# Seven stage boundaries of a twelve-layer decoder kernel joined: a stage's last norm, output and projection run inside the next stage

## The chip, the cores and the metric

The kernel runs on one core of a Trainium2 chip. The metric is device time in microseconds (us) of one execution, smaller is better. One execution was recorded by the hardware profiler. Its rows carry the time in us from the start of the recorded span.

## The reference, cut to what matters

Twelve sublayers follow each other on x, 32 sequences (batch) of 128 tokens with 128 channels, float32. Each is "x = layernorm(x + f(x))".

```python
x = _layernorm(x + _L0_ffn_ref(x, ...))      # stage 2, slots
x = _layernorm(x + _L1_attn_ref(x, ...))     # stage 3, linear attention over the batch axis
x = _layernorm(x + _L1_xattn_ref(x, ctx_768, ...))  # stage 4, 8 heads of 64
x = _layernorm(x + _L1_ffn_ref(x, ...))      # stages 5 and 5.5: rope attention, then 8 gated experts
x = _layernorm(x + _L2_attn_ref(x, ...))     # stage 6, relu attention
x = _layernorm(x + _L2_xattn_ref(x, ctx_768, ...))  # stage 7, 16 heads of 8, with an MLP
x = _layernorm(x + _L2_ffn_ref(x, ...))      # stage 8, 8 linear experts, top 2
x = _layernorm(x + _L3_attn_ref(x, ...))     # stage 9, rope attention, 16 heads of 64
x = _layernorm(x + _L3_xattn_ref(x, ctx_768, ...))  # stage 10, 16 heads of 8
x = _layernorm(x + _L3_ffn_ref(x, ...))      # stage 11, 8 gelu experts
```

Stages 0 (attention) and 1 (cross attention with a convolution) come ahead of these and are not touched. Except for stage 3, which mixes over the batch axis, and for gates that stage 11 takes from means over a sequence, a stage treats each sequence by itself: its first pair of sequences needs nothing of the last pair of the stage before.

## The kernel before, in words

All of x stays on the chip in the tile `X`, 128 partitions by 32 sequences by 128. The engines work through a stage in units: a pair of sequences (index p, 16 pairs) in `attention8`, `attention64_rope`, `attention64_cross` and `experts_gated`, four sequences (index u or v, 8 units) in `slots`, `attention_linear`, `attention_relu`, `experts_linear` and `experts_gelu`. One function writes one stage: stage 2 is `slots`, 3 `attention_linear`, 4 `attention64_cross`, 5, 7 and 10 `attention8`, 5.5 `experts_gated`, 6 `attention_relu`, 8 `experts_linear`, 9 `attention64_rope`, 11 `experts_gelu`. (In the profile tile names have lost their number: L_ffn is any of L0_ffn to L3_ffn, so the time tells the stage.)

The order of work is written out by hand. Each stage opens a block (`nc.Block()`), and in it one Python function for each engine issues that engine's instructions in program order, with waits on semaphores where another engine's result is needed. An engine runs strictly through its own list. Inside a stage the loops are software pipelined: while TensorE (PE) does unit u, the output of unit u-1 goes through residual, statistics, root and normalisation. The typical end of a unit is: PE projects the output, VectorE (DVE) adds the residual (`residual`) and takes mean and variance (`statistics`), GpSimd (POOL) takes the reciprocal root (`root`, `normed`), and either POOL writes X, or DVE makes the shift (`shifted`) and ScalarE (ACT) writes X (`block_out`). The event `x_out` counts the written units.

At the end of a block all engines meet. Then `Signals.new_stage` (L52) clears the semaphores and has a second meeting (`all_engine_barrier`, L56), the stage's memory is given back, and the next stage begins with nothing in flight. Its head is: PE transposes the first unit of X (`turn`), ACT moves the transposed unit from PSUM (`evict_x`), PE projects it, and so on. Stages 3 and 4 are already joined: they lie in one block with semaphores and memory of both, stage 3's tail (`TurnedTail`) is issued inside stage 4.

Weights lie in two buffers that alternate by stage. The queue of SyncE (SP) loads the next stage's weights during a stage (`load_weights`, L379): at the stage's start in most, but in stages 2, 3 and 6 only when the stage's last output projection is done:

```python
            def _(sp):
                sp.wait_ge(y_ps, UNITS)
                k.load_weights(sp, k.next_stage(stage))
```

so that the weights of stage 3 and of stage 7 are fetched at the very end of stages 2 and 6.

## Time and profile before

| | us |
|---|---|
| median of 3 runs | 3188.23 |
| lowest and highest | 3179.7, 3191.69 |
| profiled execution, its own time | 3196.24 |
| its recorded span | 3194.4 |
| PE busy (31745 matmuls) | 2708.6, 85% of the span |
| DVE busy | 1930.6, 60% |
| ACT busy | 1378.5, 43% |
| POOL busy | 1366.7, 43% |
| TensorE clock granted, mean of the span | 0.897 of full speed |

How to read it: busy time is summed over the engine's instructions; the granted clock has two levels, 0.5 (1.2 GHz) and 1.0 (2.4 GHz), and a mean lies between. The profiled execution lasted 8 us longer than the median run. "SPq" is the queue from which transfers are started, and in a row of the timeline the last bracket says how long the engine had been idle and what ended that.

### The profile page before, as it was taken

What the parts mean: (1) busy time and instruction counts of PE and PEld (TensorE: products, weight loads), DVE (VectorE), ACT (ScalarE), POOL (GpSimd) and SP (SyncE); (2) the same over time, 40 slices, a digit from 0 to 9 for tenths busy, and PEclk for the clock granted to TensorE, in tenths of its full rate; (3) what the DMA queues carried; (4) which work ended last, traced back from release to release, by engine and by line L of the source; (5) the groups of instructions that cost most, each with busy time, mean ns of one, the idle gap of its engine ahead of it and who ended that gap; (6) DMA issues with size and microseconds to landing.
All of it is one profiled execution on the core that took longest, in us unless ns stands there. A gap on an engine that the chain in (4) does not pass through costs nothing. (4 is left out here: it accounts for less than half of the span.)

```text
span 3194.4 us, 78319 instructions
## 1 busy us (share of the span) xinstructions
PE 2708.6 (85%) x31745; PEld 1921.9 (60%) x31745; DVE 1930.6 (60%) x5041; ACT 1378.5 (43%) x3100; POOL 1366.7 (43%) x1474
## 2 busy tenths in 40 slices
PE   7884666676689997998999976998889999979986
PEld 4552343354446775665999965666367777755665
DVE  6887999255764444665544444664856666635665
ACT  4453565263445653444322223553134444435554
POOL 4773665173301213453233333453833434335556
PEclk8996776687779998999899986997989999989998
DMA  3000000400000001000000000001000000000000
GB/s 105 2 2 1 1 1 1 117 1 1 7 19 17 2 2 41 2 3 9 1 1 1 1 1 17 2 2 44 1 6 2 2 3 2 2 9 2 2 3 25
DMA packets 25797, 37.16 MB, mean 12 GB/s; under 512 B 760, under 2 KB 22656, under 8 KB 24576
## 3 DMA queue, kind: packets, MB, share of 16 engines
q1 hardware_dynamic: 25440, 32.16, 3.3%
q8 instruction: 254, 4.16, 0.6%
q14 instruction: 103, 0.84, 0.1%
HBM read 29.93 MB, written 2.23 MB: 10 GB/s over the span
## 5 line engine op out<-in xcount | busy, mean ns | idle before, releaser
L1460 POOL TENSOR_TENSOR L_attn__qk<-L_attn__turned 128x512 f32<-128x512 f32 x128 | 161.7, 1274 | 303.1 <-DVE L_attn__turned L1571 303.1
L1024 DVE TENSOR_REDUCE L_xattn__nm<-psum 128x8 bf16<-128x1024 f32 x128 | 156.4, 1224 | 148.8 <-PE psum L1225 142.4
L4510 PE MATMUL psum<-L_ffn__e_hT,weights 128*128 128x256 f32 x1024 | 244.7, 382 | 0.0
L1571 DVE TENSOR_TENSOR L_attn__turned<-psum,weights 128x1024 f32<-128x1024 f32 x128 | 153.3, 1218 | 95.1 <-PE psum L1678 92.1
L4510 PEld LDWEIGHTS psum<-L_ffn__e_hT,weights 128*128 128x128 f32 x1024 | 186.7, 192 | 20.5
L4364 DVE TENSOR_TENSOR L_ffn__e_a<-L_ffn__e_sg,psum 128x512 f32<-128x512 f32 x128 | 88.0, 687 | 176.5 <-ACT L_ffn__e_sg L4356 176.4
L4356 ACT ACTIVATE L_ffn__e_sg<-psum 128x512 f32<-128x512 f32 x128 | 76.4, 597 | 258.7 <-PE psum L4510 258.7
L959 ACT ACTIVATE L_xattn__pT<-psum 128x1024 f32<-128x1024 f32 x128 | 124.0, 1021 | 59.3 <-PE psum L1253 59.3
L4523 PEld LDWEIGHTS psum<-weights,L_ffn__e_a 128*128 128x128 f32 x1024 | 134.3, 191 | 7.3 <-DVE L_ffn__e_a L4364 0.7
L1678 PE MATMUL psum<-L_attn__xT,weights 128*128 128x256 f32 x512 | 136.8, 401 | 2.0 <-DVE L_attn__turned L1571 1.3
L4523 PE MATMUL psum<-weights,L_ffn__e_a 128*128 128x128 f32 x1024 | 135.1, 275 | 0.5 <-DVE L_ffn__e_a L4364 0.5
L1506 ACT ACTIVATE L_attn__qk<-L_attn__qk 128x512 bf16<-128x512 f32 x128 | 77.3, 630 | 87.7 <-POOL L_attn__qk L1460 87.7
L4283 POOL TENSOR_TENSOR L_ffn__e_half<-L_ffn__e_prod 128x512 f32<-128x512 f32 x32 | 40.7, 1270 | 171.6 <-DVE L_ffn__e_prod L4373 171.6
L1024 DVE TENSOR_REDUCE L_ffn__nm<-psum 128x8 bf16<-128x1024 f32 x64 | 78.2, 1224 | 55.5 <-PE psum L1225 55.5
L954 ACT ACTIVATE L_attn__pT<-L_attn__pT,L_attn__sc 128x1024 f32<-128x1024 f32 x64 | 73.0, 1149 | 76.4 <-DVE L_attn__pT L1036 76.4
L1678 PEld LDWEIGHTS psum<-L_attn__xT,weights 128*128 128x128 f32 x512 | 90.9, 193 | 24.4 <-issue 9.9
L3040 DVE MATCH_REPLACE8 L_xattn__front_left<-L_xattn__front_top,L_xattn__front_left 128x128 f32<-128x128 f32 x384 | 100.8, 275 | 0.0
L1024 DVE TENSOR_REDUCE L_attn__nm<-psum 128x8 bf16<-128x1024 f32 x64 | 77.9, 1220 | 29.1 <-PE psum L1225 29.1
L1580 DVE TENSOR_REDUCE L_attn__nm<-psum 128x8 bf16<-128x1024 f32 x64 | 75.4, 1219 | 26.5 <-PE psum L1709 25.8
L3182 PE MATMUL psum<-L_xattn__front_diag,L_xattn__front_ex 128*128 128x128 f32 x256 | 55.6, 388 | 40.0 <-POOL L_xattn__front_ex L2869 38.7
L1529 ACT ACTIVATE L_attn__pT<-psum 128x1024 f32<-128x1024 f32 x64 | 62.0, 1021 | 62.1 <-PE psum L1738 62.1
L1900 POOL TENSOR_TENSOR L_xattn__rstd<-L_xattn__mv,eps 128x2 f32<-128x2 f32 x16 | 3.1, 194 | 198.4 <-DVE L_xattn__mv L2029 198.4
(682 smaller groups left out, 7562.1 us busy)
## 6 DMA issues: line engine op xcount, KB each, us to landing
L_xattn__conv_toeplitz<-s4d_kernel SPq DMA_DIRECT2D x5, 1024.0 KB, 12.1
weights<-pack SPq DMA_DIRECT2D x1, 3328.0 KB, 11.0
weights<-pack SPq DMA_DIRECT2D x1, 3140.0 KB, 10.1
weights<-s4d_kernel SPq DMA_DIRECT2D x3, 1024.0 KB, 9.2
L_attn__bias_tables<-pack SPq DMA_DIRECT2D x1, 2048.0 KB, 10.1
out_dram<-X SPq DMA_DIRECT2D x8, 256.0 KB, 2.3
weights<-pack SPq DMA_DIRECT2D x1, 1603.5 KB, 14.1
ctxT<-ctxT_in SPq DMA_DIRECT2D x1, 1536.0 KB, 11.0
```

What stands on the lines that cost most here:

```text
L959: nc.scalar.activation(unit, scores[u], ACT.Exp, scale=scale).then_inc(p_sb, 1)
L1024: nc.vector.tensor_reduce(nm[:, n % 2, :].rearrange("p (g c) -> p g c", g=4)[:, 2 * u:2 * u + 2, 0:4], scores[u].rearrange("p g (i q) -> p ...
L1460: nc.gpsimd.tensor_tensor(qk[:, p % 2, u], turned[:, g % 2, :, 0:2 * P], turned[:, g % 2, :, 2 * P:4 * P], ALU.add).then_inc(qk_sb, 1)
L1506: nc.scalar.activation(qk16[:, p % 2, u], qk[:, p % 2, u], ACT.Copy).then_inc(qk16_sb, 1)
L1571: nc.vector.tensor_tensor(turned[:, g % 2], proj[u % 2].unsqueeze(1).to_broadcast([P, 2, 4 * P]), k.w(name + "rope").rearrange("p (t q) -> ...
L1580: nc.vector.tensor_reduce(nm[:, n % 2, :].rearrange("p (g c) -> p g c", g=4)[:, 2 * u:2 * u + 2, 0:4], scores[u].rearrange("p g (j q) -> p ...
L1678: last = nc.tensor.matmul(proj[place % 2][:, 2 * P * t:2 * P * t + 2 * P], w[:, P * c:P * c + P], xT[:, p % 2, :], start=True, stop=True)
L3040: last = nc.vector.match_replace(left[:, u % 2, j, h, :], top[:, u % 2, j, h, 8 * r:8 * r + 8], source(u, r, j, h), 2 * NEG)
L4356: nc.scalar.activation(sg[:, g % 2, :], gate[g % 2], ACT.Silu).then_inc(sg_sb, 1)
L4364: nc.vector.tensor_tensor(a[:, g % 2].rearrange("p c s q -> p (c s q)"), sg[:, g % 2, :], up[g % 2], ALU.mult).then_inc(a_sb, 1)
L4510: last = nc.tensor.matmul(bank[g % 2][:, 256 * c:256 * c + 256], k.w(name + w)[:, o:o + P], hT, start=True, stop=True)
L4523: last = nc.tensor.matmul(Y[s][e // 4][:, P * (e % 4):P * (e % 4) + P], a[:, g % 2, c, s, :], k.w(name + "Wd")[:, P * (2 * e + c):P * (2 * ...
```

## The change

Three blocks now hold the stages: 2, 3 and 4; 5, 5.5, 6 and 7; 8, 9, 10 and 11. That joins seven boundaries: 2 to 3, 5 to 5.5, 5.5 to 6, 6 to 7, 8 to 9, 9 to 10 and 10 to 11. Those from 1 to 2, 4 to 5 and 7 to 8 keep their meetings. A joined stage returns an object `Ending` with its last piece of work for each engine as functions (`late_pe`, `late_dve`, `last_dve`, `late_act`, `late_pool`), and the next stage calls them at chosen places in its own lists. `Ending` also says on what the next stage must wait: `x_out` for a unit of X (`wait_x`), `banks_read` before it writes PSUM banks that the old stage still uses, `weights_read` before SP loads over the old weights. All waits on a unit of X are new in these stages. Memory of successive stages is taken from alternate ends (`other_end`), so that both stages' tiles can be alive; some tiles are declared in another order for that. In `experts_linear` two PSUM banks are chosen otherwise, with one more wait.

```diff
+    def other_end(self):
+        self.end = "right" if self.end == "left" else "left"
+        return self.end
...
-            return ctx.enter_context(nc.sbuf_tensor(f"{name}_{what}", shape, dt))
+            return ctx.enter_context(nc.sbuf_tensor(f"{name}_{what}", shape, dt, side=side))
...
+class Ending:
+    def __init__(self, x_out, pairs_each, weights_read, banks_read=None):
+        self.x_out, self.pairs_each, self.weights_read, self.banks_read = x_out, pairs_each, weights_read, banks_read
+
+    def wait_x(self, eng, pair):
+        eng.wait_ge(self.x_out, pair // self.pairs_each + 1)
...
@@ attention8 (stages 5, 7, 10) @@
                 nc.gpsimd.memset(nm[:], 0.0)
                 nc.gpsimd.memset(vz[:], 0.0).then_inc(zeroed, 1)
+                if before:
+                    before.late_pool(pool)
                 pool.wait_ge(k.loaded[stage], 16)
...
                 evict_v(0)
+                if before:
+                    before.late_act(act)
                 evict_x(1)
...
                     nc.vector.tensor_copy(bvw[:], k.w(name + "bv").to_broadcast([P, P])).then_inc(bv_sb, 1)
+                    if before:
+                        before.late_dve(dve)
                     dve.wait_ge(bv_ps, 1)
...
                 project_v(0)
-                if opening:
+                if before:
+                    before.late_pe(pe)
+                    pe.wait_ge(*before.banks_read)
+                if opening or before:
                     value_bias()
                 turn(1)
...
+                def late_pe(pe):
+                    if mlp:
+                        hide(LAST, LAST + 1)
+                    project_out(LAST, LAST + 1)
...
@@ attention64_rope (stage 9) @@
                 nc.gpsimd.memset(nm[:], 0.0).then_inc(zeroed, 1)
                 for u in range(UNITS):
+                    if u == 4:
+                        before.late_pool(pool)
                     add_turned(0, u)
...
                 for u in range(UNITS):
                     cast(0, u)
+                before.late_act(act)
+                act.wait_ge(before.x_out, NB // 4)
                 for i in range(4):
                     evict_v(0, i)
...
@@ attention_linear (stage 3) @@
                 for u in BY_ACT:
+                    if u == 5:
+                        before.late_act(act)
...
                 for u in BY_DVE:
+                    if u == 2:
+                        before.last_dve(dve)
...
@@ attention_relu (stage 6) @@
                 biased(0)
+                before.late_dve(dve)
...
@@ experts_gated (stage 5.5) @@
                 for u in range(UNITS):
                     rms_root(u)
+                    if u == 1:
+                        before.late_pool(pool)
...
+                before.late_dve(dve)
                 for u in range(UNITS):
                     rms_normed(u)
+                    if u == 0:
+                        before.last_dve(dve)
...
                 pe.wait_ge(k.loaded[stage], 16)
+                before.late_pe(pe)
                 turn(0)
...
@@ experts_gelu (stage 11) @@
-                for u in range(UNITS):
+                turn(0)
+                before.late_pe(pe)
+                for u in range(1, UNITS):
                     turn(u)
...
@@ the stages @@
         with k.one_block():
-            tail = attention_linear(k, 3, "L1_attn_")
+            ending = slots(k, 2, "L0_ffn_")
+            tail = attention_linear(k, 3, "L1_attn_", ending)
             attention64_cross(k, 4, "L1_xattn_", tail)
+        with ExitStack() as mid, k.one_block():
+            M = mid.enter_context(nc.sbuf_tensor("L1_ffn_mid", [P, NB, DM], F32))
+            ending = attention8(k, 5, "L1_ffn_", grouped=M, followed=True)
+            ending = experts_gated(k, 5.5, "L1_ffn_", M, ending)
+            ending = attention_relu(k, 6, "L2_attn_", ending)
+            attention8(k, 7, "L2_xattn_", cross=True, mlp=True, before=ending)
+        with k.one_block():
+            ending = experts_linear(k, 8, "L2_ffn_")
+            ending = attention64_rope(k, 9, "L3_attn_", ending)
+            ending = attention8(k, 10, "L3_xattn_", cross=True, before=ending, followed=True)
+            experts_gelu(k, 11, "L3_ffn_", ending)
```

On POOL at the boundary from stage 9 to stage 10, the list before (the first five rows write the last pair of X, `nm` and `vz` are tiles of stage 10, `k16m` is the first operand that its scores need):

```order
L1466 TENSOR_TENSOR L_attn__rstd<-L_attn__mv,eps 128x2
L1468 TENSOR_TENSOR L_attn__rstd<-L_attn__rstd,neg_half 128x2
L1472 TENSOR_SCALAR X<-L_attn__res,L_attn__mv,L_attn__rstd 128x128 x2
L1446 UNCONDITIONAL_BRANCH
L55 ISA
L776 UNCONDITIONAL_BRANCH
L848 MEMSET L_xattn__nm 128x256
L849 MEMSET L_xattn__vz 128x2560
L783 TENSOR_TENSOR L_xattn__k16m<-L_xattn__kT,const 128x1024
```

and now:

```order
L773 UNCONDITIONAL_BRANCH
L847 MEMSET L_xattn__nm 128x256
L848 MEMSET L_xattn__vz 128x2560
L1505 TENSOR_TENSOR L_attn__rstd<-L_attn__mv,eps 128x2
L1507 TENSOR_TENSOR L_attn__rstd<-L_attn__rstd,neg_half 128x2
L1511 TENSOR_SCALAR X<-L_attn__res,L_attn__mv,L_attn__rstd 128x128 x2
L780 TENSOR_TENSOR L_xattn__k16m<-L_xattn__kT,const 128x1024
```

The zeroing has moved ahead of the old stage's last norm, and `k16m` still stands behind that norm.

On PE at the same boundary, before (`rd` is the old stage's last reciprocal, spread out; `oT` its last output):

```order
L1768 MATMUL psum<-L_attn__rd,weights 128x128 x8
L1775 MATMUL psum<-weights,L_attn__oT 128x128 x8
L1446 UNCONDITIONAL_BRANCH
L1149 UNCONDITIONAL_BRANCH
L1313 MATMUL psum<-weights,L_xattn__bvw 128x128
L1160 MATMUL psum<-const,X 128x128 x2
L1172 MATMUL psum<-ctxT,weights 128x256
L1173 MATMUL psum<-L_xattn__xT,weights 128x256
L1199 MATMUL psum<-weights,ctxT 128x128 x2
L1160 MATMUL psum<-const,X 128x128 x2
```

and now:

```order
L1828 MATMUL psum<-L_attn__rd,weights 128x128 x8
L1171 UNCONDITIONAL_BRANCH
L1184 MATMUL psum<-const,X 128x128 x2
L1196 MATMUL psum<-ctxT,weights 128x256
L1197 MATMUL psum<-L_xattn__xT,weights 128x256
L1223 MATMUL psum<-weights,ctxT 128x128 x2
L1835 MATMUL psum<-weights,L_attn__oT 128x128 x8
L1337 MATMUL psum<-weights,L_xattn__bvw 128x128
L1184 MATMUL psum<-const,X 128x128 x2
```

The old stage's last projection (reading `oT`) has moved behind the new stage's first transposes and projections.

On ACT at the boundary from stage 8 to stage 9, before:

```order
L4629 ACTIVATE L_ffn__wT<-psum 32x128
L4634 ACTIVATE X<-L_ffn__r,L_ffn__shift,L_ffn__rstd 128x128 x12
L4578 UNCONDITIONAL_BRANCH
L1493 UNCONDITIONAL_BRANCH
L1500 ACTIVATE L_attn__xT<-psum 128x256
L1506 ACTIVATE L_attn__qk<-L_attn__qk 128x512 x8
L1512 ACTIVATE L_attn__v<-psum 128x512 x4
```

and now:

```order
L4789 ACTIVATE L_ffn__wT<-psum 32x128
L4794 ACTIVATE X<-L_ffn__r,L_ffn__shift,L_ffn__rstd 128x128 x4
L1538 UNCONDITIONAL_BRANCH
L1545 ACTIVATE L_attn__xT<-psum 128x256
L1551 ACTIVATE L_attn__qk<-L_attn__qk 128x512 x8
L4794 ACTIVATE X<-L_ffn__r,L_ffn__shift,L_ffn__rstd 128x128 x8
L1557 ACTIVATE L_attn__v<-psum 128x512 x4
```

Eight writes of X, two units of stage 8, now stand between the casts of `qk` and the moves of `v` out of PSUM.

## Rows read from the trace of the kernel before

**Rows 1.** Windows, seven boundaries: stretch, us; busy PE, PEld, DVE, ACT, POOL; PEclk, DMA, GB/s

```profile
849.10:855.30 6.20, 0.00 (x0) 0.02 (x1) 2.00 (x10) 2.95 (x8) 1.24 (x3) 0.50 0.28 77
1502.50:1512.30 9.80, 0.69 (x5) 0.56 (x5) 3.78 (x8) 3.72 (x24) 3.54 (x6) 0.72 0.19 54
1871.30:1882.60 11.30, 0.00 (x0) 0.00 (x0) 4.25 (x12) 0.00 (x0) 7.33 (x10) 0.68 0.00 0
1965.00:1971.40 6.40, 0.00 (x0) 0.00 (x0) 2.35 (x11) 2.66 (x7) 1.70 (x4) 0.50 0.30 82
2309.10:2321.30 12.20, 0.01 (x1) 0.04 (x1) 4.84 (x14) 3.29 (x8) 6.34 (x9) 0.63 0.00 1
2854.00:2864.90 10.90, 3.79 (x17) 3.49 (x17) 2.41 (x6) 1.09 (x2) 2.99 (x6) 0.55 0.00 0
3068.30:3076.40 8.10, 0.69 (x5) 0.55 (x5) 3.31 (x7) 0.00 (x0) 2.80 (x5) 0.82 0.00 0
```

**Rows 2.** Window, the boundary from stage 3 to 4, joined already

```profile
967.40:977.40 10.00, 7.69 (x39) 5.28 (x38) 5.14 (x17) 6.23 (x14) 3.87 (x6) 1.00 0.12 51
```

**Rows 3.** Timeline, stage 2 to 3: start us, us, engine line op out<-in xcount [idle before <-releaser]

```profile
849.12 0.34 SPq L383 DMA_DIRECT2D weights<-pack  x1
...
852.59 1.65 ACT L3748 ACTIVATE X<-L_ffn__r,L_ffn__shift,L_ffn__rstd 128x128 f32<-128x128 f32 x4 [2.19 <-DVE L_ffn__shift L3912]
...
857.35 4.65 ACT L2530 ACTIVATE L_attn__HT<-psum,weights 128x128 f32<-128x128 f32 x16 [3.12 <-PE psum L2671]
```

**Rows 4.** DMA issues, weights of stage 7 and of stage 3: KB, us to landing

```profile
weights<-pack SPq DMA_DIRECT2D x1, 514.5 KB, 3.5
...
weights<-pack SPq DMA_DIRECT2D x1, 469.0 KB, 3.7
```

**Rows 5.** Timeline, stage 5 to 5.5, DVE

```profile
1502.57 1.76 DVE L1043 RECIPROCAL L_ffn__rd<-psum 128x256 f32<-128x256 f32 x1 [3.23 <-PE psum L1275]
...
1511.01 2.42 DVE L4409 SCALAR_TENSOR_TENSOR L_ffn__e_xn<-L_ffn_mid,L_ffn__e_ms,weights 128x128 f32<-128x128 f32 x8 [4.94 <-POOL L_ffn__e_ms L4314]
```

**Rows 6.** Timeline, stage 5.5 to 6: DVE's last residual, and PE's first state product

```profile
1877.28 0.29 DVE L4383 TENSOR_TENSOR L_ffn__e_total<-L_ffn__e_moe,L_ffn_mid 128x128 f32<-128x128 f32 x1 [1.22 <-POOL L_ffn__e_moe L4291]
...
1890.79 1.16 PE L2383 MATMUL psum<-L_attn__kv,L_attn__kr 128*128 128x128 f32 x8 [1.18 <-POOL L_attn__kr L2228]
```

**Rows 7.** Timeline, stage 6 to 7: SP's two loads of weights, PE's first transposes

```profile
1964.99 6.25 SPq L383 DMA_DIRECT2D weights<-pack  x2
...
1972.30 0.67 PE L1160 MATMUL psum<-const,X 128*128 128x128 f32 x2
```

**Rows 8.** Timeline, stage 8 to 9: POOL's last sum, its last first-pair add, ACT's moves of v

```profile
2313.68 0.73 POOL L4594 TENSOR_TENSOR L_ffn__quarter<-L_ffn__half 128x256 f32<-128x256 f32 x1
...
2335.57 1.26 POOL L1460 TENSOR_TENSOR L_attn__qk<-L_attn__turned 128x512 f32<-128x512 f32 x1 [0.18 <-DVE L_attn__turned L1571]
...
2337.40 1.06 ACT L1512 ACTIVATE L_attn__v<-psum 128x512 f32<-128x512 f32 x2
```

**Rows 9.** Timeline, stage 9 to 10: last projection, last write of X, first k16m

```profile
2856.09 3.78 PE L1775 MATMUL psum<-weights,L_attn__oT 128*128 128x128 f32 x16 [2.09 <-DVE L_attn__oT L1596]
...
2861.93 1.57 POOL L1472 TENSOR_SCALAR X<-L_attn__res,L_attn__mv,L_attn__rstd 128x128 f32<-128x128 f32 x2
...
2869.46 1.89 POOL L783 TENSOR_TENSOR L_xattn__k16m<-L_xattn__kT,const 128x1024 bf16<-128x1024 f32 x1 [2.51 <-ACT L_xattn__kT L910]
```

**Rows 10.** Timeline, stage 10 to 11: last write of X, and the step behind the last transpose

```profile
3073.79 1.57 POOL L813 TENSOR_SCALAR X<-L_xattn__res,L_xattn__mv,L_xattn__rstd 128x128 f32<-128x128 f32 x2
...
3084.22 0.18 DVE L4920 TENSOR_SCALAR L_ffn__pooled<-L_ffn__total 128x32 f32<-128x32 f32 x1
```

**Rows 11.** Windows: router of stage 5.5, transposes of stage 11

```profile
1522.00:1536.00 14.00, 14.00 (x60) 13.28 (x61) 7.15 (x65) 4.94 (x14) 1.99 (x3) 0.50 0.00 1
...
3076.40:3080.30 3.90, 3.90 (x18) 3.29 (x19) 1.72 (x3) 1.91 (x4) 0.00 (x0) 0.50 0.00 0
3080.30:3082.80 2.50, 2.37 (x16) 1.49 (x14) 2.29 (x5) 2.27 (x4) 0.00 (x0) 1.00 0.00 0
```

314 lines of the change are left out of this document (192 added, 122 removed).

## The prediction

> **What bounds the kernel now.** I read the page's busy times first: PE works 85% of the span and no other engine more than 60%, so over most of the time an interruption of PE is lost time. I then laid the timeline over each place where one stage ends and the next begins, and asked the view by windows how much PE does there. [rows 1] gives the seven stretches that the change touches, from the end of PE's main work in the old stage to PE's start in the new one. They last 6.2, 9.8, 11.3, 6.4, 12.2, 10.9 and 8.1 us, 64.9 us together, and PE works 5.2 us of them. The reader should see that the other engines work only about a third of each stretch too: what fills it is a chain, in which each engine waits for the one before it. These 60 idle us are 1.9% of the time, and they bound what bridging can give. The boundary from stage 3 to stage 4, joined already, looks otherwise: in the 10 us around it PE works 7.69 us, at full clock [rows 2].
>
> **The change, boundary by boundary.** It removes no arithmetic. It removes two meetings at each boundary, and puts the old stage's last chain beside the new stage's first unit. The time from the last write of X to the new stage's start is what the meetings cost: 852.59 + 1.65 = 854.24 to 855.3 [rows 1, 3], so 1.0 us, and about the same at each, 7 us in all. The rest depends on which wait ends last in the new head. I follow each head to the first step that the following work hangs on, with its old durations, and compare.
>
> *2 to 3.* PE can begin its transposes at 849.1 instead of 855.3. But stage 3's weights are asked for only at 849.12 [rows 3] and take 3.7 us [rows 4], so ACT and DVE, which wait for them before they take anything from PSUM, start at 852.8. ACT has 4 units of 4 moves, 4.65 us [rows 3], and now the last write of X, 1.65 us, between its second and third. It ends at 852.8 + 4.65 + 1.65 = 859.1 instead of 862.0. **2.9 us.** Before, this load was hidden by the chain and the meetings; now it is what comes last.
>
> *5 to 5.5.* The reciprocal ends at 1504.33 [rows 5], the product after it takes some 0.4 us, and then DVE does the new stage's first unit, 4 of the 8 operations in 2.42 us, 1.2 us [rows 5]. PE transposes from 1506.0 or 1506.1 instead of 1512.3 [rows 1]. The second DVE unit has the residual ahead of it (0.4 us), and POOL's third root has the old stage's last clip (about 1 us) ahead. From 6.2 us I take those off in part: **5.5 us.**
>
> *5.5 to 6.* PE is free at 1871.3 and nothing in stage 6's first unit needs the last pair. Before, PE began at 1882.6 [rows 1] and reached the product that needs POOL's result at 1890.79 [rows 6], 8.2 us later. Now that is 1879.5. A second limit is POOL, which is busy with the old stage's expert sums until the time at which DVE takes them, 1877.28 [rows 6], and then needs some 1.5 us for the new stage's positive part: 1878.8, not later. DVE's old residual waits for the same sums, but stands behind the bias of unit 0. **11.3 us**, the whole stretch.
>
> *6 to 7.* Stage 7's weights are asked for at 1964.99 [rows 7] and take 3.5 us [rows 4]. PE waits for them even ahead of its first transposes, which stood at 1972.3 (some 0.2 us earlier by their weight load) and now stand at 1968.5. The old last residual on DVE also waits for these weights now, since it stands behind DVE's wait, but by my estimate root and write are done by 1977, about where the shifted head next needs ACT. **3.6 us.**
>
> *8 to 9.* PE has nothing late and starts at 2309.1. POOL is the brake: its expert sums end at 2314.41 [rows 8], and only then come the first pair's eight adds, 1.26 us each [rows 8], which feed ACT's casts. In the old head they ran to 2336.83, about 10.9 us from the first start (their turned operands come from DVE at the same pace). DVE's late residual and statistics fall between its fourth and fifth, which I price at 2.5 us, half of what DVE does in the stretch [rows 1]. So the adds end at 2314.8 + 10.9 + 2.5 = 2328.2, 8.6 us earlier. Then ACT has two units of X to write, 2 x 1.65 us by [rows 3], before it moves v, on which PE waits. Before, they had been written ahead of the stage. 8.6 - 3.3 = **5.3 us.**
>
> *9 to 10.* This is the place where most is given back. PE starts the new head at 2854.0. In the old head the step `k16m` on POOL came at 2869.46 [rows 9], 4.6 us after PE's start at 2864.9 [rows 1]; so the operands would be there at 2858.7. But PE now does the old projection here, 3.78 us, to 2862.5, and from the end of that projection to the end of POOL's write of X it took 2859.87 to 2863.50, 3.6 us [rows 9]. POOL has that norm ahead of `k16m`, which therefore starts at 2866.1 instead of 2869.46. **3.4 us** out of 10.9.
>
> *10 to 11.* Stage 11 needs all of X, transposed, before its gates. The last pair is still written at 3075.36 [rows 10], but now all other transposes are done by then. Last transposes 1 us, ACT's move 0.6, DVE's sum 0.7 and small gaps: the pooled mean at 3077.9 instead of 3084.22 [rows 10]. **6.3 us.** The rest of stage 11 is shifted as it is.
>
> Sum: 2.9 + 5.5 + 11.3 + 3.6 + 5.3 + 3.4 + 6.3 = **38.3 us**. The added waits (on X, banks and weights) mostly find their event past, and queue nothing but what is counted above. SP's wait on `weights_read` in stages 5.5, 7, 9 and 10 moves loads by a few us that are needed one stage later, 80 us and more away; I cost it at nothing. So do I cost the other memory ends, the tiles' order and the other banks of stage 8: no address appears in a row, and the arithmetic is the same. Against the profiled execution the sum gives 3196.24 - 38.3 = 3157.9 us. That execution stands 8.0 us over the median, so the forecast is 3188.23 - 38.3 = **3150 us**.
>
> **The clock, the cost that the sum leaves out.** The mean granted clock in the seven stretches is 0.50 to 0.82 [rows 1], and it is where 0.5 is 1.2 GHz. In the router of stage 5.5 PE is busy for all of 14 us at 0.5 [rows 11], so the idle stretch ahead is not all that holds it down. At the joined boundary it is 1.0 [rows 2]. If the bridging keeps the clock up, a head's PE time halves at best: 14 us become 7 there. From both sides: nothing gained (the old durations hold, as in my sum), or up to half of some 60 busy us in the heads, of which other engines allow perhaps two thirds, 20 us. I take nothing, because the stretches at 2 to 3 and 6 to 7 are at 0.50 from end to end [rows 1]: there the clock was down already while PE still had work, and not because of the boundary.
>
> The Trainium skill, on the page "TensorE: Matmul & The Clock Gate", in "Part 4: PE-mode transpose", says that the full clock does not engage for transposes, since they are not counted as PE work. By that the transposes that the change puts first into the idle stretches could not hold the clock, and this extra gain would be near nothing. The trace speaks otherwise: in stage 11's head only transposes run from 3076.4 to 3082.8, and the clock is 0.5 up to 3080.3 and 1.0 after [rows 11]. So I leave the extra gain a chance of its own.
>
> **Rivals.**
> A, *the clock stays up*: for it speaks the joined boundary [rows 2], against it the router. 10 to 20 us more than the sum, some 3135 us. By the same page's section "HAM oscillation — how this bites in real kernels", idle gaps of PE are what brings the clock down; this would make A likely.
> B, *the lists give more back*: an engine runs its own list in order, and a late step that waits holds all of the new head behind it, as at 9 to 10. If 5.5 to 6 and 8 to 9 do the same (DVE's old residual waits for POOL there, the adds wait for DVE), 11.3 and 5.3 become 3.4 each as in the case worked out, 10 us less, and with a few us more at the others the gain is 20 to 28 us: 3164 us.
> C, *it doesn't do what it says*: the head cannot start before the last X after all, and only the meetings go, 7 x 1.0 us: 3181 us, no measurable change.
> D, *slower*: the long stretches at full clock are what the kernel lives on; mean 0.897 means that some 20% of the span is at 0.5. If another spacing of the heads drops a long phase (stage 9 is the longest) to 0.5, each such us costs up to half a us. To cancel 38 us takes 77 us more at 0.5, and from 110 us on, about 17% more than now, it is slower by over 16 us: 3205 us. Nothing in the steady loops changes, so this is unlikely.
>
> **How the numbers follow.** Forecast 0.60, A 0.18, B 0.13, C 0.06, D 0.03. About 0.5%, 16 us, is what a measurement of this kernel can tell from no change, so the bound of faster is 3172 us; forecast, A and nearly all of B lie under it: faster 0.90, same 0.08, slower 0.02. The range takes in the forecast with the spread of runs (12 us over three), A's 20 us on one side and B on the other: 3130 to 3168 us.
>
> **What would show it.** In the new profile the gap of PE should be under 3 us at 5.5 to 6, and 3 to 4 us around the weights' landing at 2 to 3 and 6 to 7, with ACT and DVE released by a DMA there. `k16m` at 9 to 10 should be released by POOL's own norm, and ACT's eight writes of X should stand ahead of its first move of v. Stages from head to head should be as long as before. I am wrong if stages get longer by what their heads gain, or if the granted clock moves by more than 0.01.

## The result, and the profile after

The changed kernel takes 3163.34 us, the median of four runs (3160.22 to 3166.35), against 3186.93 us for the kernel before (four runs, 3179.7 to 3191.69). The ratio is 0.9927, with a 95% interval of 0.991 to 0.9945: 23.6 us, or 0.7%, faster. The forecast was 38.3 us. The profiled execution lasted 3162.29 us, its span 3160.5 us, at a mean granted clock of 0.908 (before: 3196.24, 3194.4 and 0.897). Its span is 33.9 us shorter than that of before, more than the medians are apart; 8.8 us of this lie in stages 0 and 1, whose code is the same in both.

The page after, the busy line and the granted clock in 40 slices:

```profile
PE 2699.9 (85%) x31745; PEld 1918.1 (61%) x31745; DVE 1929.2 (61%) x5041; ACT 1378.0 (44%) x3100; POOL 1365.7 (43%) x1474
...
PEclk9997767787779998999899997997989999999998
```

The busy sums say little: PE 2699.9 us instead of 2708.6, the other engines the same within 1.5 us. No work went away, as the change says. To see where the time went I cut both executions at the same instructions. A boundary reaches from the start of the last but one residual on DVE in the old stage to the start of the second residual in the new one (in stage 5.5 the ninth of the `L_ffn__e_a` products from either end). The same matmuls lie in a boundary before and after, so its length splits into two parts that can be compared one by one: PE's busy time, which for the same matmuls only the clock and the waits inside them change, and PE's idle time, which is what a joined boundary is to remove.

The view by windows of the kernel **before**, the boundaries 2 to 3, 3 to 4, 5 to 5.5, 5.5 to 6, 6 to 7, 8 to 9, 9 to 10 and 10 to 11 (stretch, us; busy PE, PEld, DVE, ACT, POOL; PEclk, DMA, GB/s):

```profile
843.92:966.94 123.02, 90.02 (x698) 48.97 (x699) 73.28 (x230) 51.31 (x134) 14.23 (x15) 0.78 0.07 21
971.36:1005.77 34.41, 32.01 (x306) 23.31 (x306) 13.86 (x31) 22.43 (x44) 2.88 (x5) 1.00 0.01 2
1498.90:1557.60 58.70, 49.48 (x364) 46.12 (x365) 24.42 (x106) 22.00 (x85) 12.26 (x18) 0.74 0.04 10
1848.42:1908.11 59.69, 43.90 (x244) 37.45 (x242) 23.24 (x55) 11.51 (x21) 22.50 (x27) 0.87 0.00 1
1959.98:2024.61 64.63, 49.65 (x592) 32.50 (x592) 28.57 (x48) 28.89 (x63) 25.55 (x22) 0.70 0.07 22
2305.74:2376.99 71.25, 52.39 (x623) 35.74 (x622) 41.72 (x58) 24.23 (x45) 29.97 (x29) 0.86 0.02 6
2844.86:2913.07 68.21, 50.59 (x751) 34.32 (x751) 26.51 (x35) 25.76 (x55) 24.52 (x21) 0.80 0.03 9
3064.71:3114.27 49.56, 38.41 (x305) 32.42 (x305) 30.35 (x64) 24.05 (x40) 26.16 (x26) 0.93 0.01 2
```

and the same eight in the **changed** kernel:

```profile
835.09:961.78 126.69, 98.40 (x698) 52.22 (x699) 72.36 (x229) 51.06 (x134) 14.18 (x15) 0.73 0.06 20
966.21:1002.22 36.01, 33.60 (x306) 24.70 (x306) 13.86 (x30) 22.43 (x44) 2.88 (x5) 0.95 0.01 2
1492.57:1545.18 52.61, 48.98 (x364) 45.74 (x364) 24.27 (x106) 22.00 (x85) 11.85 (x18) 0.77 0.04 11
1836.00:1885.25 49.25, 42.18 (x243) 36.69 (x243) 23.00 (x55) 11.51 (x21) 22.49 (x27) 0.95 0.00 1
1937.15:1998.48 61.33, 48.83 (x592) 32.07 (x592) 29.91 (x47) 28.89 (x63) 25.41 (x22) 0.74 0.08 23
2282.07:2355.12 73.05, 56.03 (x623) 38.13 (x622) 40.60 (x57) 24.14 (x45) 29.88 (x29) 0.84 0.02 6
2822.27:2886.62 64.35, 49.83 (x751) 33.92 (x750) 26.30 (x34) 25.85 (x55) 21.93 (x19) 0.84 0.03 10
3038.27:3081.13 42.86, 36.43 (x305) 30.96 (x305) 30.02 (x64) 23.73 (x40) 26.16 (x26) 1.00 0.01 3
```

The reader should see the first two numbers behind the stretch, and the clock. At 2 to 3 the same 698 matmuls took 90.02 us at 0.78 and then 98.40 us at 0.73, so PE worked 8.4 us longer; its idle time, 123.02 - 90.02 = 33.0 us, became 28.3 us. Taken so for all:

| boundary | forecast gain | PE idle | PE busy | together |
|---|---|---|---|---|
| 2 to 3 | 2.9 | -4.7 | +8.4 | +3.7 |
| 3 to 4 (joined already) | none | 0.0 | +1.6 | +1.6 |
| 5 to 5.5 | 5.5 | -5.6 | -0.5 | -6.1 |
| 5.5 to 6 | 11.3 | -8.7 | -1.7 | -10.4 |
| 6 to 7 | 3.6 | -2.5 | -0.8 | -3.3 |
| 8 to 9 | 5.3 | -1.8 | +3.6 | +1.8 |
| 9 to 10 | 3.4 | -3.1 | -0.8 | -3.9 |
| 10 to 11 | 6.3 | -4.7 | -2.0 | -6.7 |
| sum | 38.3 | -31.2 | +7.9 | -23.3 |

In this pair of profiles idle time fell by 31.2 us in the eight boundaries and PE's busy time rose by 7.9. Between the boundaries the stages are as long as before, within 0.7 us in all but stage 8, which took 51.4 us instead of 49.2 (below). Of the two boundaries that keep their meetings, 7 to 8 took 64.6 us for 64.4 and 4 to 5 68.4 for 71.2. The 7.9 us are no fixed price of the change: a second profile of the same changed kernel (e8, below) has 1.9 us less busy time in these boundaries than before. And only one execution of the kernel before was profiled, one that lasted 9.3 us longer than the median of the four.

**The head of stage 9** is the boundary that missed its forecast by most, 7.1 us: it became longer. Timeline, stage 8 to 9, changed kernel (start us, us, engine line op out<-in xcount [idle before <-releaser]):

```profile
2290.02 0.72 POOL L4750 TENSOR_TENSOR L_ffn__quarter<-L_ffn__half 128x256 f32<-128x256 f32 x1
2290.69 0.31 POOL L1515 MEMSET L_attn__nm<- 128x256 bf16 x1
2291.10 2.29 DVE L1664 CAST L_attn__masks<-weights 128x4096 bf16<-128x4096 f32 x1 [4.74 <-POOL L_attn__nm L1515]
...
2294.61 2.49 POOL L1499 TENSOR_TENSOR L_attn__qk<-L_attn__turned 128x512 f32<-128x512 f32 x2 [3.61 <-DVE L_attn__turned L1619]
...
2309.11 1.26 POOL L1499 TENSOR_TENSOR L_attn__qk<-L_attn__turned 128x512 f32<-128x512 f32 x1 [0.44 <-DVE L_attn__turned L1619]
...
2310.94 3.17 ACT L4794 ACTIVATE X<-L_ffn__r,L_ffn__shift,L_ffn__rstd 128x128 f32<-128x128 f32 x8
2314.14 1.08 ACT L1557 ACTIVATE L_attn__v<-psum 128x512 f32<-128x512 f32 x2
```

Read it from the top. POOL ends stage 8's last expert sum at 2290.74 and only then comes to the new stage's zeroing (MEMSET). DVE's cast of the masks waits 4.74 us for that zeroing, and behind the cast in DVE's list stand the turned operands, for which POOL's adds and PE's projections wait. The adds run from 2294.61 to 2310.37. Then ACT writes eight blocks of X, 3.17 us, and moves v, on which PE waits, only at 2314.14. That is 28.8 us after PE's first transposes (2285.32), which follow the end of its old work directly, where the kernel before had its v at 28.3 us after the end of PE's work [rows 1, 8].

The granted clock of the same head, by windows:

```profile
2285.35:2293.00 7.65, 2.40 (x11) 1.60 (x10) 2.92 (x3) 0.38 (x1) 5.41 (x8) 1.00 0.00 0
2293.00:2299.80 6.80, 5.13 (x12) 3.71 (x12) 5.22 (x7) 1.70 (x3) 3.80 (x4) 0.50 0.00 0
```

Up to 2293 PE worked 2.40 of 7.65 us and waited for the rest; then the clock is 0.5 for 6.8 us, and again from 2303.2 to 2310.0, from 2313.5 to 2320.3 and from 2323.7 to 2327.1. The first three falls lie in gaps of PE of 6.4, 3.1 and 4.1 us. In the whole boundary PE was busy for 20.0 us at half clock, and before for 10.4 us, though the half clock itself lasted nearly as long then, 20.5 us (2312.3 to 2326.0 and 2343.0 to 2349.8) against 23.8: 9.0 us of it lay in the old idle stretch, where PE did nothing. These 9.6 us more of work at half clock cover the 3.6 us of added busy time.

### The profile page after: what moved, and what is told of

Read it like the earlier page. It is cut to its first block and busy times, and to the rows that moved or that the text cites. A ratio compares the mean times of both kernels' runs of the same rounds, so it can differ in the third digit from the quotient of the medians.

```text
span 3160.5 us, 78251 instructions
## 1 busy us (share of the span) xinstructions
PE 2699.9 (85%) x31745; PEld 1918.1 (61%) x31745; DVE 1929.2 (61%) x5041; ACT 1378.0 (44%) x3100; POOL 1365.7 (43%) x1474
```

## The experiments

The table holds what the profiles of all kernels show. Each kernel is the changed one with the edit named; the text below calls a boundary "joined and unedited" where it is as the change has it. A pair is PE idle + PE busy in us at that boundary, worked out as above; the last two columns are the sums over the eight boundaries.

```
profile                     2 to 3        6 to 7        8 to 9        9 to 10       idle   busy
before                      33.0 + 90.0   15.0 + 49.6   18.9 + 52.4   17.6 + 50.6   123.0  406.4
changed kernel              28.3 + 98.4   12.5 + 48.8   17.0 + 56.0   14.5 + 49.8    91.9  414.3
e1_cast_free                29.7 + 86.5   12.5 + 48.8   15.1 + 54.8   14.5 + 46.6    91.4  395.8
e2_apart_8_9                27.9 + 97.7   12.4 + 48.8   18.6 + 51.5   14.1 + 48.9    92.2  407.9
e3_apart_2_3                33.4 + 86.4   12.5 + 48.9   17.1 + 54.9   14.5 + 46.5    97.3  397.9
e4_weights_early            27.8 + 88.7    9.4 + 48.6   17.0 + 56.0   14.5 + 49.8    88.2  404.3
e5_k16_first                27.3 + 95.2   14.3 + 49.3   17.2 + 55.7    9.8 + 47.1    87.6  409.0
e6_act_between_casts        28.2 + 98.3   12.5 + 48.8   12.3 + 50.8   14.5 + 46.5    87.1  405.7
e7_all_four                 26.8 + 95.3   11.0 + 49.1   13.6 + 51.7   10.1 + 49.0    81.1  404.5
e8_change_again             28.9 + 93.9   12.5 + 48.8   17.0 + 56.0   14.5 + 46.7    92.5  404.5
e9_norm_first_in_7          27.5 + 89.0    9.4 + 48.5   12.3 + 50.8   10.0 + 47.5    78.8  394.8
e10_and_2_3_apart           33.0 + 86.6    9.4 + 48.5   12.3 + 50.8   10.1 + 47.0    84.0  395.0
```

The idle columns repeat from kernel to kernel within 1.3 us wherever the code is the same (2 to 3 within 2.4). The busy columns do not. The kernels of e1 to e6 were timed in a single execution each. Nine executions of the changed kernel lie between 3158.38 and 3171.25 us, so one time says little of an edit worth a few us, and the boundaries are read instead.

### e1: the cast of the masks free of POOL's zeroing

```diff
                 dve.wait_ge(k.loaded[stage], 16)
-                dve.wait_ge(zeroed, 1)
                 nc.vector.tensor_copy(
...
                         before.last_dve(dve)
+                dve.wait_ge(zeroed, 1)
                 maxima(0)
```

> Edit: in stage 9 DVE no longer waits for POOL's zeroing of nm before it casts the masks; the wait stands before its first maxima instead. The stretch from stage 8's last-but-one residual to stage 9's second residual was 71.2 us before the change and is 73.1 us after it. Theory one (the cast, held back behind POOL's expert sums, delays the first turned operands): 69 to 71 us, 2 to 4 us less than 73.1. Rival (PE at half clock and ACT's two late units of X pace the head): 72.5 to 73.5 us.

Measured: 3149.09 us in one execution (before in the same job 3191.68). The boundary 8 to 9 took 69.9 us instead of 73.1. Timeline, the same head:

```profile
2279.60 2.52 DVE L1663 CAST L_attn__masks<-weights 128x4096 bf16<-128x4096 f32 x1
...
2280.05 2.66 POOL L4750 TENSOR_TENSOR L_ffn__quarter<-L_ffn__half 128x256 f32<-128x256 f32 x1
...
2299.46 1.26 POOL L1499 TENSOR_TENSOR L_attn__qk<-L_attn__turned 128x512 f32<-128x512 f32 x1 [0.44 <-DVE L_attn__turned L1619]
...
2304.49 1.08 ACT L1557 ACTIVATE L_attn__v<-psum 128x512 f32<-128x512 f32 x2
```

DVE casts at 2279.60, about 1 us after PE's first transposes (2278.64), instead of 5.8 us after them. The adds end at 2300.72, 22.1 us after the transposes; in the changed kernel it was 25.1. Windows, 8 to 9:

```profile
2275.39:2345.28 69.89, 54.77 (x623) 36.76 (x622) 40.74 (x58) 24.13 (x45) 31.74 (x29) 0.85 0.02 6
```

What follows: the wait for the zeroing, behind POOL's expert sums, held the adds back by 3.0 us and cost 2 to 3 us of the missing gain. Idle time fell by 1.9 us; the other 1.2 us are busy time, 54.8 us, and without this edit that lay between 54.9 and 56.0. The whole 38.3 us is not back by this, though the profile's span, 3147.3 us, is 13.2 us under that of the changed kernel: 10.4 us of that lie at 2 to 3, where nothing was edited. The second row shows something else: POOL's quarter sum, 0.73 us otherwise, took 2.66 us. It started 0.45 us into the cast and ended 0.59 us after it (2282.12), and it took 2.66 us in all five kernels that have the cast free. The Trainium skill has this on the page "SBUF — State Buffer", in "Who interferes with whom": of DVE in a 2-port performance mode and GpSimd, whoever issues first has a shared pair of ports for the whole instruction, and the other blocks fully. Which mode the cast ran in no row shows; the times agree with the rule: POOL lost 1.9 us, less than the 3.0 us by which the adds came earlier.

### e2: boundary 8 to 9 in two blocks again

```diff
-            ending = experts_linear(k, 8, "L2_ffn_")
-            ending = attention64_rope(k, 9, "L3_attn_", ending)
+        experts_linear(k, 8, "L2_ffn_", followed=False)
+        with k.one_block():
+            ending = attention64_rope(k, 9, "L3_attn_", None)
```

> Edit: the boundary from 8 to 9 alone is put back to two blocks; all else as after the change. If the join itself costs there (late ACT, late DVE and the cast in the new head), the stretch from 8 to 9 goes back to 71.2 us and the kernel gets 2 us faster. If the longer stretch is only the clock's phase in that one execution, it comes out 71 to 75 us without relation to the join. Stage 8's own body was 49.2 us before and 51.4 after with other PSUM banks, which this kernel keeps: if the banks cost, its body is 51.4 again; if the clock, it may be anything from 49.2.

Measured: 3168.38 us in one execution. 8 to 9 took 70.1 us, against 72.0 to 73.1 in the five profiles that have it joined and unedited. Idle time is 18.6 us (joined 17.0 to 17.2), busy time 51.5 us (joined 54.9 to 56.0). That is under both ranges named. What follows: joining this boundary as the change does it made it 2 to 3 us longer. It removes 1.5 us of idle time and adds some 4 us of busy time: PE was busy for 8.4 us at half clock here, as before (10.4) and not as joined (20.0). This rests on two profiles in two blocks against five joined. The kernel as a whole did not get the 2 us faster that were expected, its one time lies among those of the changed kernel. Stage 8 itself took 51.4 us here, with the new banks; but it took 49.2 us in three other profiles with the same new banks (e3, e5, e7), as in the kernel before with the old ones, so the banks are not what makes the difference.

### e3: boundary 2 to 3 in two blocks again

```diff
-            ending = slots(k, 2, "L0_ffn_")
-            tail = attention_linear(k, 3, "L1_attn_", ending)
+        slots(k, 2, "L0_ffn_", followed=False)
...
+            tail = attention_linear(k, 3, "L1_attn_", None)
```

> Edit: the boundary from 2 to 3 alone is put back to two blocks. From stage 2's last-but-one residual to stage 3's second it took 123.0 us before and 126.7 after, where I had forecast 120.1. Theory one (transposes that run early no longer warm PE up right before stage 3's real work, and PE is at half clock for its first 17 us): 122 to 124 us here, with the clock at full within 5 us of the first transposes. Rival (stage 3's clock swings at random and costs up to 5 us in any run): 123 to 128 us here too.

Measured: 3156.49 us in one execution, and the boundary took 119.8 us, under the ranges of both theories. Windows, 2 to 3:

```profile
841.94:961.78 119.84, 86.43 (x698) 47.33 (x699) 72.94 (x230) 51.29 (x134) 14.24 (x15) 0.82 0.07 22
```

Idle time is 33.4 us, as before the change (33.0): joining removes 5 us of it. But PE's busy time is 86.4 us here, 86.5 in the kernel with the cast free and 98.4 in the changed kernel, the latter two with the same code at this place. So the early transposes alone do not keep PE at half clock there, as the first theory had it: with them the busy time can be as low as without. What follows is in the section on e10, which looks at it again with more runs.

### e4: the weights of stages 3 and 7 asked for earlier

Stage 2 asks for stage 3's weights at its start, and stage 6 for stage 7's as soon as the old weights have been read:

```diff
-                sp.wait_ge(y_ps, UNITS)
+                sp.wait_ge(*before.weights_read)
                 k.load_weights(sp, k.next_stage(stage))
...
-                sp.wait_ge(y_ps, UNITS)
                 k.load_weights(sp, k.next_stage(stage))
```

> Edit: stage 3's weights are loaded at the start of stage 2, and stage 7's at the start of stage 6, behind the old stage's last read of that buffer. Theory one (the landing is the wait that ends last at both heads): the stretch 6 to 7 falls from 61.3 to 57.5 to 58.5 us, and 2 to 3 by 1 to 3 us from 126.7. Rival (behind the weights the last write of X, or POOL's root, is as late): 6 to 7 falls by less than 1.5 us, 2 to 3 by less than 1 us.

Measured: 3153.08 us in one execution. Windows, 6 to 7:

```profile
1931.16:1989.10 57.94, 48.56 (x592) 32.10 (x592) 31.80 (x47) 28.78 (x63) 25.39 (x22) 0.76 0.05 15
```

6 to 7 took 57.9 us instead of 61.3, with 9.4 us idle instead of 12.5: the landing of the weights held this head for 3.1 us, as the prediction had it. 2 to 3 took 116.4 us, 10.3 less than in the changed kernel where 1 to 3 were expected, but the kernel with the cast free, without this edit, took 116.3 there. By idle time, the three kernels with the edit have 27.8, 26.8 and 27.5 us, the six joined ones without it 27.3 to 29.7, mean 28.4: about 1 us, at the edge of what can be told.

### e5: the masked keys ahead of the old norm

Stages 7 and 10 mask their first keys and queries on POOL before they do the old stage's late norm:

```diff
-                if before:
-                    before.late_pool(pool)
                 pool.wait_ge(k.loaded[stage], 16)
...
                     mask_keys(0)
                     mask_queries(0)
+                    if before:
+                        before.late_pool(pool)
                     pool.wait_ge(bo_sb, 1)
```

> Edit: in stages 7 and 10 POOL makes the first pair's k16m and qm before the old stage's last norm instead of after it. After the change k16m of stage 10 started 11.5 us after PE's first transposes there, 7.2 us after its operand kT was ready. Theory one (POOL's list order gives this time back, as forecast): the stretch from 9 to 10, 64.3 us after the change and 61.1 to 64.3 in the runs so far, falls to 57 to 60.5 us; k16m starts 4.5 us behind the first transposes, and what comes last is then PE's own late projection ahead of its rough scores. Rival (PE's late projection and DVE's bias are as late anyway): 61 to 64 us.

Measured: 3153.68 us in one execution. Windows, 6 to 7 and 9 to 10, then the timeline of the second:

```profile
1935.13:1998.73 63.60, 49.28 (x592) 32.07 (x592) 28.80 (x47) 28.78 (x63) 25.39 (x22) 0.73 0.07 22
2820.19:2877.04 56.85, 47.10 (x751) 31.48 (x749) 26.30 (x35) 25.73 (x55) 21.93 (x19) 0.91 0.04 11
```

```profile
2829.26 0.44 PE L1184 MATMUL psum<-const,X 128*128 128x128 f32 x2
...
2832.64 1.89 POOL L780 TENSOR_TENSOR L_xattn__k16m<-L_xattn__kT,const 128x1024 bf16<-128x1024 f32 x1 [23.81 <-ACT L_xattn__kT L917]
```

`k16m` starts 3.4 us after PE's first transposes, where the changed kernel had 11.5 (below) and 4.5 were expected. 9 to 10 lost 4.7 us of idle time (14.5 to 9.8) and took 56.8 us instead of 61.1 to 64.3. At 6 to 7 the same edit cost: 63.6 us instead of 61.3, idle 14.3 instead of 12.5. The late norm is not needed soon in stage 10's head, but in stage 7's it may be (e9 tests it).

### e6: ACT's late writes of X between its casts

The kernel with the cast free, and of ACT's two late units one ahead of its fifth cast and one ahead of its eighth:

```diff
                 for u in range(UNITS):
+                    if u == 4:
+                        before.first_act(act)
+                    if u == 7:
+                        before.late_act(act)
                     cast(0, u)
-                before.late_act(act)
```

> Edit: the cast of the masks does not wait for POOL, as in the first of these runs, and ACT writes stage 8's last two units of X between its casts (the sixth unit after the fourth cast, the seventh before the last) instead of after the eighth. The stretch from 8 to 9 was 69.9 us with the cast alone. Theory (ACT's 3.2 us stand straight in the way of the moves of v): 67 to 68 us. Rival (PE at half clock sets the pace of the head): 69.5 to 70.5 us.

Measured: 3153.6 us in one execution. Windows, 8 to 9, then the timeline around the last add:

```profile
2285.49:2348.58 63.09, 50.82 (x623) 34.37 (x622) 40.75 (x57) 23.92 (x45) 31.77 (x29) 0.92 0.03 7
```

```profile
2309.57 1.26 POOL L1499 TENSOR_TENSOR L_attn__qk<-L_attn__turned 128x512 f32<-128x512 f32 x1 [0.44 <-DVE L_attn__turned L1622]
2309.70 1.63 ACT L4797 ACTIVATE X<-L_ffn__r,L_ffn__shift,L_ffn__rstd 128x128 f32<-128x128 f32 x4
...
2311.76 1.05 ACT L1557 ACTIVATE L_attn__v<-psum 128x512 f32<-128x512 f32 x2
```

ACT moves v at 2311.76, 0.9 us after the end of the last add (2310.83). In the kernel with the cast free it was 3.8 us after it (2300.72 to 2304.49), and in the changed kernel too (2310.37 to 2314.14). The boundary took 63.1 us instead of 69.9, 4 us below the range of the theory: idle 12.3 instead of 15.1, busy 50.8 instead of 54.8. So the 3.3 us that the prediction took off for ACT were real, and avoidable. PE's busy time fell too, by 4.0 us, and that repeats: e7, e9 and e10 have this edit and 51.7, 50.8 and 50.8 us. The granted clock in the three stretches of 10 us from 2300 is 0.50, 1.00 and 1.00, where in the kernel with the cast free it is 0.50, 0.67 and 0.82 in those from 2290. With both edits the boundary is 8.2 us shorter than before the change, where 5.3 were forecast.

### e7 and e8: all four edits, and the change once more, in one job

> All four edits together on the changed kernel: free cast, ACT's writes between the casts, weights of stages 3 and 7 early, k16m first. If the gains add (3.2 + 2.3 at 8 to 9, 3.4 at 6 to 7, 4.2 at 9 to 10, and 0 to 5 at 2 to 3), it is 13 to 18 us faster than the changed kernel of the same job and 37 to 42 us faster than the kernel before. If clock phases eat them, less than 8 us over the changed kernel.

> The changed kernel again, nothing edited: one more sample of each stage's length, and its time in the same rounds. If the differences between runs in stages 3, 8 and around 9 are the clock's phase, then the stretch 2 to 3 comes out anywhere in 116 to 127 us, while the stretches 5 to 5.5, 5.5 to 6, 6 to 7 and 10 to 11 repeat within 0.3 us (52.6, 49.2, 61.3, 42.9). Total 20 to 30 us under the kernel before.

Measured in the same job: all four 3147.04 us (four runs, 3144.21 to 3150.55), ratio to before 0.9867 (0.9849 to 0.9885); the change 3164.76 us (five runs, 3158.38 to 3171.25), ratio 0.9928 (0.9912 to 0.9944); before 3187.63 us (nine runs). The four edits together are worth 17.7 us on top of the change, within the 13 to 18 us expected, and the result of the change is confirmed by fresh runs. Place by place, against the first profile of the change, the gains did not add as named: 8 to 9 gave 7.7 us for 5.5, 6 to 7 1.2 for 3.4 (e9 says why) and 9 to 10 5.2 for 4.2. Of the stretches that should repeat within 0.3 us in e8, three did, and 5 to 5.5 took 52.2 us for 52.6. The fastest run of the change, 3158.38 us, had a mean granted clock of 0.907, the slowest, 3171.25 us, 0.901; but another at 0.907 took 3163.67 us. The profile of that fastest run has 92.5 us of idle time and 404.5 us busy in the eight boundaries; the first profile of the same kernel had 91.9 and 414.3. Idle time repeats; busy time differs by 10 us with nothing changed.

### e9 and e10: the norm first in stage 7, and 2 to 3 apart

Two versions, both with the four edits, but with the masked keys first in stage 10 alone:

```diff
+                if before and stage != 10:
+                    before.late_pool(pool)
...
+                    if before and stage == 10:
+                        before.late_pool(pool)
```

> The kernel of the four edits, but with the masked keys ahead of the norm's late units in stage 10 alone; stage 7 has them as the change has. In the two profiles with the edit in both stages the boundary 6 to 7 took 2.3 us more than beside them without it (63.6 to 61.3, 60.2 to 57.9). Theory one: in stage 7 the late units of the norm lie on the way to the residuals of unit 0 or 1, so the order costs there what it gains in stage 10: 6 to 7 back to 57.9 us, 9 to 10 as in the four edits' profile, 59.2 or below, and the time 2 us below 3147, some 3145 us. Rival: the 2.3 us come from the clock's phase, and 6 to 7 stays at 60.2 us.

> The kernel just before, with the boundary 2 to 3 back in two blocks (stage 3's weights still asked for at the start of stage 2). Theory one: over the profiles so far the joined boundary took 116.3 to 126.7 us (mean of eight 121.9) and the one in two blocks 119.8 and 123.0, so joining it is worth nothing that can be told from where the clock's halves fall: the time is within 3 us of the kernel just before in the same job. Rival: joining is worth the 2.9 us of the forecast or more, and this kernel is 3 to 6 us slower than the one just before.

(The nine joined profiles, this one included, run from 116.3 to 126.7 us; the mean of the eight ahead of it is 122.4, not the 121.9 of the expectation.)

Measured: 3140.32 us for the first (four runs, 3135.97 to 3143.77), ratio 0.986 (0.9841 to 0.988), and 3137.37 us for the one with 2 to 3 apart (five runs, 3132.22 to 3149.65), ratio 0.9853 (0.9828 to 0.9877). Windows of the first, 2 to 3 and 6 to 7, and of the second, 2 to 3:

```profile
838.70:955.19 116.49, 88.95 (x698) 48.31 (x699) 73.00 (x229) 51.12 (x134) 14.20 (x15) 0.81 0.06 19
1931.14:1988.97 57.83, 48.45 (x592) 32.06 (x592) 31.82 (x47) 28.81 (x63) 25.41 (x22) 0.76 0.05 15
```

```profile
837.38:957.02 119.64, 86.63 (x698) 48.29 (x699) 73.26 (x229) 51.77 (x134) 14.24 (x15) 0.82 0.06 18
```

6 to 7 is back at 57.8 us, idle 9.4: in stage 7 it was the order of the list that cost, not the clock. The time is 6.7 us below that of e7. 6 to 7 explains 2.3 us of it, and 2.2 us are the job: the kernel before took 3185.42 us in this one and 3187.63 in that of e7. The rest lies within the scatter of runs. 2 to 3 apart has 33.0 us idle and 86.6 busy, joined 27.5 and 89.0; and the two kernels' times cannot be told apart, 2.95 us with runs that scatter over 8 and 17 us. Over all profiles the joined boundary has 26.8 to 29.7 us idle and 86.5 to 98.4 busy (nine, mean 93.7), in two blocks 33.0 to 33.4 idle and 86.4 to 90.0 busy (three, mean 87.7). So joining 2 to 3 surely removes 5 us of idle time. That the clock always takes it back is not shown, with three profiles against nine; on the mean it took 6.

Either version is 45 to 48 us faster than the kernel before in the same job. The change ran in other jobs; by the ratios to the kernel before the two are some 22 to 24 us faster than it.

## Why the prediction was right, and where it was wrong

**The size of the gain: wrong by 15 us, inside the range.** The forecast was 3150 us and the time is 3163.3. In the profiles five boundaries gave 30.4 us where 30.1 were forecast. The miss lies at the other two: 2 to 3 and 8 to 9 became 5.5 us longer instead of 8.2 us shorter, and 3 to 4, for which nothing was forecast, 1.6 us longer. Split the other way, idle time fell by 31.2 us of 38.3 and busy time rose by 7.9. The first part repeats in e8 (30.5 us less idle), the second does not (1.9 us less busy), so how much of the missing gain the clock took in the median run is not shown. The time is where rival B put it (3164 us), but B's own places were half wrong: it had 5.5 to 6 giving 3.4 us, which gave 10.4, and 8 to 9 giving 3.4, which gave nothing. That the number agrees is luck for the most part.

**2 to 3: the term right, the clock against it.** The weights do come last:

```profile
840.29 0.35 SPq L380 DMA_DIRECT2D weights<-pack  x1
...
843.88 2.28 ACT L2640 ACTIVATE L_attn__HT<-psum,weights 128x128 f32<-128x128 f32 x8 [2.30 <-DMA weights<-pack]
...
849.88 2.05 PE L2804 MATMUL psum<-L_attn__HT,weights 128*128 128x512 f32 x2 [1.60 <-ACT L_attn__HT L2640]
```

They land 3.6 us after SP asked for them, ACT and DVE are released by the DMA, as the signs said, and ACT's fourth unit is done at 849.7, 9.4 us after SP's request; before it was 12.9 us [rows 3], so 3.4 us came off, where 2.9 were forecast. But then PE's first two products took 2.05 us, instead of 1.10. Windows of the changed kernel from 0.8 us ahead of these products, and of the kernel before from 0.8 us ahead of its own (862.15):

```profile
849.10:866.20 17.10, 15.22 (x74) 7.41 (x75) 7.77 (x24) 5.40 (x16) 1.26 (x1) 0.50 0.00 1
```

```profile
861.34:878.44 17.10, 11.50 (x103) 5.96 (x103) 10.78 (x31) 8.12 (x23) 2.53 (x2) 1.00 0.00 1
```

For 17.1 us the changed kernel ran at 0.50 with PE busy for 15.2 of them, and did 74 matmuls. The kernel before ran at 1.00 and did 103, busy for 11.5 us. The step that failed is the one on the clock: "nothing gained" at one end, "up to half of some 60 busy us in the heads" at the other, and "I take nothing". It bounded the clock from one side alone. A loss was possible too, at 2 to 3 of 8.4 us and at 8 to 9 of 3.6 us. The second repeats in the five joined and unedited profiles (2.5 to 3.6 us); the first does not, in another profile of the same code it was a gain of 3.5 us (e1).

**5 to 5.5: right.** 6.1 us for 5.5.

**5.5 to 6: right.**

```profile
1864.81 1.50 POOL L2300 TENSOR_SCALAR L_attn__kr<-L_attn__kv 128x512 f32<-128x512 f32 x1
...
1866.36 2.08 PE L2477 MATMUL psum<-L_attn__kv,L_attn__kr 128*128 128x128 f32 x8 [3.25 <-POOL L_attn__kr L2300]
```

POOL's positive part (`kr`) ended at 1866.31, 7.6 us after PE's first transposes of the new stage (1858.69); the forecast had 7.5 as the limit and 8.2 for the product, and the product came at 7.7. PE waited 3.25 us for it, a little over the 3 us that were named as the sign. 10.4 us for 11.3.

**6 to 7: right, and shown by an experiment.**

```profile
1942.15 4.92 SPq L380 DMA_DIRECT2D weights<-pack  x2
...
1945.91 0.69 PE L1184 MATMUL psum<-const,X 128*128 128x128 f32 x2 [3.79 <-DMA weights<-pack]
```

PE waited 3.79 us for the weights, which came 3.7 us after SP's request (3.5 forecast), and the boundary gave 3.3 us for 3.6. With the weights there earlier it gave 3.4 us more (e4).

**8 to 9: wrong, by the largest amount.** The step that failed is "so the adds end at 2314.8 + 10.9 + 2.5". It took POOL's sums as the only brake on the first add and let DVE do its head freely. DVE's cast, though, waits for a zeroing that POOL issues behind those sums; before, the same wait cost nothing, because POOL came to the stage with an empty list. Counted from PE's first transposes, the adds began at 9.3 us instead of 5.7, and ended at 25.1 instead of 19.1. With the cast free it was 7.6 (2286.21 to 2278.64) and 22.1. So of the 6.0 us by which the adds ended late the cast is 3.0. DVE's late piece took 3.1 us (2299.61 to 2302.69) where 2.5 were priced, and in waits of 1.10, 0.48 and 0.41 us DVE stood for PE's projections at half clock. The 3.3 us for ACT's late writes were right (3.17 in the row). The busy time that was added is half clock on work instead of on the old gap, as told above; e2 shows the boundary at 70.1 us in two blocks and at 73 joined. The prediction had also read that the other engines work only about a third of each stretch. For POOL that is wrong just here: it works 6.34 of 12.2 us at 8 to 9, and 7.33 of 11.3 at 5.5 to 6 [rows 1]. It was POOL's list that held the zeroing back.

**9 to 10: right in kind.**

```profile
2831.34 0.44 PE L1184 MATMUL psum<-const,X 128*128 128x128 f32 x2
...
2841.31 1.57 POOL L1511 TENSOR_SCALAR X<-L_attn__res,L_attn__mv,L_attn__rstd 128x128 f32<-128x128 f32 x2
2842.85 1.89 POOL L780 TENSOR_TENSOR L_xattn__k16m<-L_xattn__kT,const 128x1024 bf16<-128x1024 f32 x1
```

`k16m` stands right behind POOL's own norm, as named, and starts 11.5 us after PE's first transposes, for 12.1 forecast and 15.5 before, counted there from the end of PE's main work [rows 9, with the start of rows 1]. The boundary gave 3.9 us for 3.4. Masking first removed the cause (e5): idle time fell by another 4.7 us.

**10 to 11: right.**

```profile
3047.42 1.58 POOL L812 TENSOR_SCALAR X<-L_xattn__res,L_xattn__mv,L_xattn__rstd 128x128 f32<-128x128 f32 x2
...
3051.09 0.18 DVE L5096 TENSOR_SCALAR L_ffn__pooled<-L_ffn__total 128x32 f32<-128x32 f32 x1
```

From the end of the last write of X (3049.00) to the pooled mean are 2.1 us, for 2.5 forecast and 8.9 before [rows 10]; 6.7 us for 6.3.

**Rival A**, that the clock stays up, was half right: it did at five boundaries (0.74 to 0.77, 0.87 to 0.95, 0.70 to 0.74, 0.80 to 0.84, 0.93 to 1.00, together 5.8 us less busy time) and fell at three. (A part of the higher means can be that the idle time taken out lay at half clock.) The rule of the Trainium skill that speaks against A, on the page "TensorE: Matmul & The Clock Gate", in "Part 4: PE-mode transpose", can be held against the stretch in which nearly all of PE's work is transposes, by windows of the changed kernel:

```profile
3044.88:3051.40 6.52, 3.91 (x30) 2.91 (x29) 5.74 (x13) 3.87 (x7) 2.48 (x4) 1.00 0.00 0
```

Of its 30 matmuls 28 are transposes, PE was busy for 3.91 of 6.52 us, and the clock was at 1.00 all through. As at stage 11's head before [rows 11], the trace does not bear the rule out for these transposes. The page speaks of matmuls with the transpose mode on; whether these had it on no row shows.

**C and D** are excluded: the meetings alone would have given 7 us, and no long phase of a stage lost its clock (stage 9 took 467.1 us for 467.9). Of the named signs one more is to be told: the mean clock of the span moved by 0.011, just over the 0.01 that was named. The 19 executions of the kernel before in the later jobs had 0.897 to 0.908, with a median of 0.903, and the nine of the change 0.901 to 0.908, with a median of 0.906. So most of the 0.011 is the one profile of before (0.897), which is low.

## What to carry to other kernels

When two stages are joined, walk each engine's list in its new order and ask of every wait at the new head who signals it and what that engine now has in front: a wait that was free because the signaller came with an empty list costs as much as the old tail in front of the signal. Put an old stage's late piece not at one place by habit, but behind the last step of the new head that other engines wait for, unless the next step needs its result; the same order gained 4.7 us of idle time in one stage and cost 1.6 to 1.8 in another. And compare profiles by idle and busy time of PE between the same two instructions: idle time shows the edit, within 1.3 us here (2.4 at 2 to 3), while busy time moved by 10 us with nothing changed. Idle time is not wholly free of the clock either. Up to stage 2's first residual, where the code is the same, the profile after has 12.4 us less busy time than that before (545.9 us for 558.3) and 3.5 us more idle: part of what PE saves by a faster clock shows up again as waiting.
